# Sixteen sequences of a state-space scan: fourteen of them in a hardware loop, or all sixteen written out

## The chip, the cores and the metric

The kernel runs on one core of a Trainium2 chip. The metric is the device time of one execution in microseconds (us). The core has five instruction streams that run side by side and meet only at semaphores: PE (TensorE, matmuls), DVE (VectorE), ACT (ScalarE), POOL (GpSimd) and SP (SyncE, which here only issues DMA transfers).

## The reference, cut to what matters

A batch of 16 sequences of 1024 tokens (256 features each) passes through a Mamba layer and then through an attention layer with a mixture of experts. Only the Mamba layer, the state space, is touched here:

```python
xz = einsum('bld,ed->ble', hidden_states, in_proj_w)          # 512 channels x, 512 channels z
x_conv = silu(sum(x_pad[:, w:w + L] * conv_w[:, w] for w in range(4)) + conv_b)
dt_in, Bv, Cv = split(einsum('bld,ed->ble', x_conv, x_proj_w))  # 64, 16 and 16 columns
delta = softplus(einsum('blr,dr->bld', dt_in, dt_proj_w) + dt_proj_b)
def step(h, inp):                                             # over the 1024 tokens of a sequence
    d_t, B_t, C_t, u_t = inp
    h = h * exp(d_t[:, :, None] * A) + (d_t * u_t)[:, :, None] * B_t[:, None, :]
    return h, einsum('bdn,bn->bd', h, C_t)                    # 16 states for each of 512 channels
y = (ys + x_conv * D) * silu(z)
out = x + einsum('bld,md->blm', y, out_proj_w)
```

## The kernel before, in words

Four stages follow each other with a barrier between them: `mamba_stage`, `attention_stage`, `routing_stage`, `expert_stage`. The change is in the first alone.

`mamba_stage` works on a sequence in two halves of 512 tokens, called r = 0 and 1; a pair (sequence, half) is the `q` of the code. In a half there are 32 units: two passes over 256 channels each, times 16 states. A unit holds two scans of 128 channels by 512 tokens. For a unit, SP fetches a row of B (`m_bb`) and a row of C (`m_cb` or `m_cv`), broadcast to 128 partitions; ACT makes `m_decay` = exp(delta * A) (line 524); POOL multiplies `m_du` by the row of B (`m_dbu`, line 373); DVE runs the recurrence as two scans (`m_h`, line 634), in the second half from the saved end `m_h_end` of the first; POOL (13 units of 32, line 382) or DVE (19 of 32, line 616) multiplies the state by the row of C (`m_prod`); PE adds the products up in `m_y_bank` (line 751). Four units are in flight (`RING = 4`). The projections, the convolution, the softplus and the output of the neighbouring halves are cut into small pieces and put between the units by a table (`SIDE`), on the same engines: `m_side`, `m_xc`, `m_zs`, `m_delta`, `m_xres`.

What belongs to which turn is counted by semaphores: `count(q, per_block, done)` (lines 46 to 50) gives the number that a semaphore must have reached in half q. Each engine runs the same function `sequences` (lines 233 to 238): its body once for sequence 0, then in a loop on the engine (`Fori`) for sequences 1 to 14, then once for sequence 15. In the loop b is a value in a register, so the numbers that are waited for are worked out in registers (`REGISTER_ALU` at lines 58 and 65) and so are the addresses of the transfers. For sequences 0 and 15 they are constants. Four helpers wait through `wait_apart`, which puts an increment of a semaphore that nobody reads behind the wait: all waits of SP, one of ACT (line 474) and one of DVE (line 555).

The loop is closed by a compare and a branch back to its first instruction; 14 passes have 13 such jumps back. Loop passes are entered from sequence 0 and left to sequence 15 without one. A sequence is named here by its number; it begins for DVE with the first scan whose input is not `m_h_end`.

Of the kernel before, what the change touches and what calls it, by code (L numbers as in the profile page):

```python
# [13 lines left out]
S, L, H = 16, 1024, 256  # L14
# [16 lines left out]
class Allocator:  # L31
# [11 lines left out]
    def sem(self, name):  # L43
        return self.ctx.enter_context(self.nc.semaphore(self.prefix + name))


def count(block, per_block, done):


    b, half = block  # L50
    return b * (HALVES * per_block) + (half * per_block + done)


def wait(eng, sem, value):

    if isinstance(value, int) and value <= 0:
        return
    eng.wait_ge(sem, value)


def wait_apart(eng, sem, value, passed):

    if isinstance(value, int) and value <= 0:
        return
    eng.wait_ge(sem, value)
    eng.sem_inc(passed, 1)


def mamba_stage(nc, x, w, x1, rows_bc):
# [25 lines left out]
    OUTS, PREPS = len(out_uses), len(prep_uses)  # L95
# [17 lines left out]
    def prep_done(kind, i):  # L113

        return 1 + prep_uses.index((kind, i))

    def bank_of(kind, i):
        return uses.index((kind, i)) % SIDE_BANKS
# [16 lines left out]
    with ExitStack() as ctx:  # L135
        al = Allocator(nc, ctx, "m_")
        sb, sem = al.sb, al.sem
# [47 lines left out]
        s_const = sem("const")  # L185
        s_a = sem("a")
        s_diag = sem("diag")
        dve_passed, sp_passed = sem("dve_passed"), sem("sp_passed")
        act_passed = sem("act_passed")
        x_loaded = sem("x_loaded")  # L190
        xres_loaded = sem("xres_loaded")
        x1_stored = sem("x1_stored")
# [3 lines left out]
        stats_done = sem("stats_done")  # L196
# [3 lines left out]
        prep_taken = sem("prep_taken")  # L200
# [27 lines left out]
            return (q[0], q[1] + 1) if q[1] < HALVES - 1 else (q[0] + 1, 0)  # L228

        def first(q):  # L230
            return isinstance(q[0], int) and q[0] == 0 and q[1] == 0

        def sequences(eng, body):

            body(0, False)
            with eng.Fori(1, S - 1) as b:
                body(b, False)
            body(S - 1, True)

        def unit_at(q, u):  # L240

# [11 lines left out]
        @block.sync  # L253
        def _(sp):
            def wait_then(sem_, value):
                wait_apart(sp, sem_, value, sp_passed)

            def load_x(q):
                if not first(q):
                    wait_then(ln_done, count(q, 1, 0))  # L260
                sp.dma_start(xin[:], x_blocks[q[0], q[1]]).then_inc(x_loaded, 16)
# [50 lines left out]
            def body(b, last):  # L312
                for half in range(HALVES):
                    q = (b, half)
                    ends = last and half == HALVES - 1
                    for u in range(UNITS):
                        if u + RING - 1 < UNITS or not ends:
                            load_b(*unit_at(q, u + RING - 1))
                        to, later = unit_at(q, u + 2)
                        if later in POOL_UNITS and not (ends and to is not q):  # L320
                            load_c(to, POOL_UNITS.index(later))
                        if later in VECTOR_UNITS and not (ends and to is not q):
                            load_c_for_vector(to, VECTOR_UNITS.index(later))
                        if first(q) and u + 1 in POOL_UNITS and u == 0:
                            load_c(q, 0)
                        if u == 0 and not last:
                            load_x(after(after(q)))
                        if u == 1 and not first(q):
                            load_residual(before(q))
                        if u == STORE_ROWS_AT and not ends:  # L330
                            store_rows(after(q))
                        if u == UNITS - 3 and not first(q):
                            store_result(before(q))
            sequences(sp, body)
            g = (S - 1, HALVES - 1)
            load_residual(g)
# [5 lines left out]
        def _(pool):  # L342
# [8 lines left out]
            def inverse_deviation(q):  # L351
                wait(pool, stats_done, count(q, 2, 2))
                wait(pool, ln_done, count(q, 1, 0))
                nc.gpsimd.tensor_tensor(rstd[:], moments[:, :, 1], eps[:], ALU.add).then_inc(rstd_done, 1)
                nc.gpsimd.tensor_tensor(shift[:], moments[:, :, 0], minus_one[:], ALU.mult).then_inc(rstd_done, 1)
                wait(pool, rstd_done, count(q, 4, 2))
                nc.gpsimd.tensor_tensor(rstd[:], rstd[:], minus_half[:], ALU.pow).then_inc(rstd_done, 1)
                wait(pool, rstd_done, count(q, 4, 3))
                nc.gpsimd.tensor_tensor(shift[:], shift[:], rstd[:], ALU.mult).then_inc(rstd_done, 1)
# [53 lines left out]
        def _(act):  # L413
# [57 lines left out]

            def softplus_exp(q, i):
                bank = side_bank[:, bank_of("dt", i)]
                wait_apart(act, prep_taken, count(q, PREPS, prep_done("dt", i)), act_passed)
                if i == 0:
                    nc.scalar.preload_act_table_set("natural_log_exp_and_others")
                nc.scalar.activation(bank, bank, ACT.Exp, scale=-1.0).then_inc(soft_done, 1)
# [55 lines left out]
            def body(b, last):  # L533
                for half in range(HALVES):
                    scan_block((b, half), last and half == HALVES - 1, not last)
            sequences(act, body)


        @block.vector
        def _(dve):  # L540
# [8 lines left out]
            def statistics(q):  # L549
                wait(dve, x_loaded, count(q, 16, 16))  # L550
                wait(dve, rstd_done, count(q, 4, 0))
                for j in range(TB):
                    ins = nc.vector.bn_stats(stats[:, j], xin[:, j])
                ins.then_inc(stats_done, 1)
                wait_apart(dve, stats_done, count(q, 2, 1), dve_passed)
                for j in range(TB):
                    ins = nc.vector.bn_aggr(moments[:, j], stats[:, j])
                ins.then_inc(stats_done, 1)
# [60 lines left out]
            def scan_block(q, last, norm):  # L619
                r = q[1]  # L620
                for u in range(UNITS):
                    n, slot = u % NS, u % RING
                    for cc in range(PC):
                        wait(dve, decay_done, scans_done(q, u, cc))
                        if cc == 0:
                            wait(dve, dbu_done, units_done(q, u))
                            to, earlier = unit_at(q, u - RING)
                            if not (first(q) and u < RING):
                                wait(dve, prod_by_pool, count(to, PU, pool_upto(earlier)))
                            if r:  # L630
                                wait(dve, end_saved, q[0] * UNITS + min(UNITS, UNITS - RING + u + 1))
                            else:
                                wait(dve, end_saved, q[0] * UNITS + (u - RING + 1 if u >= RING else 0))
                        nc.vector.tensor_tensor_scan(h[:, slot, cc], decay[:, cc], dbu[:, slot, cc],  # L634
                                                     h_end[:, u, cc:cc + 1] if r else 0.0,
                                                     ALU.mult, ALU.add).then_inc(scan_done, 1)
                        if cc == 0:
                            to, earlier = unit_at(q, u - 1)
                            if earlier in VECTOR_UNITS and not (first(q) and u == 0):
                                weigh_state(to, earlier)  # L640
                        finishing(q, PC * u + cc, not first(q))
                        if not last:
                            preparation(q, PC * u + cc, norm)
# [5 lines left out]
            def body(b, last):  # L649
                for half in range(HALVES):  # L650
                    scan_block((b, half), last and half == HALVES - 1, not last)
            sequences(dve, body)
            q = (S - 1, HALVES - 1)
# [1090 lines left out]
def build(nc, t, out):  # L1744


    def scratch(name, shape):
        return nc.dram_tensor(name, shape, F32, kind="Internal").ap()

    x1 = scratch("x1", (S, L, H))  # L1750
    n2 = scratch("n2", (TOKENS, H))
    logits = scratch("logits", (L // P, P, S, EXPERTS))
    info = scratch("info", (P * COLS, 2))
    rows_bc = scratch("rows_bc", (HALVES, 2, NS, T))
    mamba_stage(nc, t["x"], t, x1, rows_bc)
    attention_stage(nc, x1, t, out, n2, logits)
    with nc.sbuf_tensor("weight_row", [P, NB], I32) as weight_row:
        routing_stage(nc, logits, info, weight_row)
        expert_stage(nc, t, n2, info, weight_row, out)
# [36 lines left out]
```

## Time and profile before

| what | value |
|---|---|
| device time, median of 3 runs (lowest to highest) | 6873.41 us (6872.57 to 6882.47) |
| time of the profiled execution | 6878.51 us |
| span of the profiled execution, on which all rows stand | 6876.8 us |
| instructions executed | 90070 |
| busy: PE, POOL, DVE, ACT | 88%, 77%, 60%, 51% |
| first scan of sequence 0, of 1, of 15 on DVE | 73.75, 298.17, 3544.91 us |
| first work of DVE in the attention stage | 3787.77 us |

The profiled execution took 1.7 us more than its span and 5.1 us more than the median. The busy shares are means over four stages. The state space fills the first 3780 us or so, a little more than half of the span; the digits of the page show DVE and POOL at 9 tenths there, PE at 8 to 9 and ACT at 6 to 7.

### The profile page before, as it was taken

The numbers are of one execution on the slowest core, as the hardware profiler recorded it, in microseconds if no ns is written. First come the engines' busy times: TensorE is split into PE (matmuls) and PEld (weight loads), VectorE is DVE, ScalarE is ACT, GpSimd is POOL, SyncE is SP. The second block draws the span as 40 slices with busy tenths as digits, with TensorE's granted clock in tenths as the row PEclk, the third lists the DMA queues.
The fourth block names the chain that finished last, engine by engine and source line by source line (L and its number), as shares of the span: only waits on it lengthen the run. The fifth ranks groups of instructions, "written<-read, shape, count | busy, mean of one in ns | idle before, by whom it ended". The sixth has DMA issues, their size and how long they took to land. (4 is left out here: it accounts for less than half of the span.)

```text
span 6876.8 us, 90070 instructions
## 1 busy us (share of the span) xinstructions
PE 6057.5 (88%) x24804; PEld 3848.5 (56%) x24804; DVE 4131.6 (60%) x4999; ACT 3516.7 (51%) x6417; POOL 5285.1 (77%) x4084
## 2 busy tenths in 40 slices
PE   7999989998989998999897899930299999999999
PEld 3444434443434443444443688830288888888888
DVE  6999999989999999999998477750000000000000
ACT  6676667666666666666665688720022222222222
POOL 6999999999999999999998777637655555555554
PEclk9999999999999999999999999965699999999999
DMA  3554555555554554455554244410266666666654
GB/s 124 163 161 161 159 160 161 157 153 163 160 161 156 160 163 157 157 162 160 161 158 142 73 123 125 125 60 1 76 183 183 184 184 184 185 185 185 180 168 132
DMA packets 556960, 1030.16 MB, mean 150 GB/s; under 512 B 82546, under 2 KB 250996, under 8 KB 521904
## 3 DMA queue, kind: packets, MB, share of 16 engines
q1 hardware_dynamic: 441168, 669.34, 31.4%
q0 software_dynamic: 115296, 355.56, 17.5%
q8 instruction: 146, 2.39, 0.1%
q14 instruction: 350, 2.87, 0.1%
HBM read 926.04 MB, written 88.88 MB: 148 GB/s over the span
## 5 line engine op out<-in xcount | busy, mean ns | idle before, releaser
L373 POOL TENSOR_TENSOR m_dbu<-m_du,m_bb 128x1024 f32<-128x1024 f32 x1024 | 2395.0, 2369 | 55.3 <-DVE m_h L634 54.6
L751 PE MATMUL m_y_bank<-m_prod,m_ident 128*128 128x512 f32 x4096 | 1955.6, 606 | 157.2 <-POOL m_prod L382 153.8
L524 ACT ACTIVATE m_decay<-m_delta,m_a_neg 128x512 f32<-128x512 f32 x2048 | 1417.6, 694 | 916.0 <-DVE m_h L634 893.5
L751 PEld LDWEIGHTS m_y_bank<-m_prod,m_ident 128*128 128x128 f32 x4096 | 778.4, 193 | 1125.9 <-issue 900.5
L634 DVE TENSOR_TENSOR_SCAN m_h<-m_decay,m_dbu 128x512 f32<-128x512 f32 x1024 | 1198.2, 1210 | 107.3 <-issue 76.9
L634 DVE TENSOR_TENSOR_SCAN m_h<-m_decay,m_h_end,m_dbu 128x512 f32<-128x512 f32 x1024 | 1261.0, 1274 | 0.7
L1694 DVE TENSOR_SCALAR e_ye<-e_ybank,e_listing 128x256 f32<-128x256 f32 x270 | 118.3, 480 | 1818.7 <-PE e_ybank L1728 1818.7
L1680 ACT ACTIVATE e_a<-e_ubank 128x512 f32<-128x512 f32 x540 | 322.4, 597 | 1474.9 <-PE e_ubank L1719 1474.9
L382 POOL TENSOR_TENSOR m_prod<-m_h,m_cb 128x1024 f32<-128x1024 f32 x416 | 983.8, 2365 | 90.5 <-DVE m_h L634 83.2
L1719 PE MATMUL e_ubank<-e_xT,e_w 128*128 128x256 f32 x4320 | 979.5, 380 | 1.3 <-ACT e_xT L1671 1.3
L1728 PE MATMUL e_ybank<-e_w,e_a 128*128 128x256 f32 x4320 | 954.5, 379 | 0.7 <-ACT e_a L1680 0.7
L1728 PEld LDWEIGHTS e_ybank<-e_w,e_a 128*128 128x128 f32 x4320 | 820.7, 190 | 112.6 <-ACT e_a L1680 1.1
L1719 PEld LDWEIGHTS e_ubank<-e_xT,e_w 128*128 128x128 f32 x4320 | 812.2, 191 | 107.1 <-issue 1.6
L1624 POOL DMA_INDIRECT e_w<-in_w,weight_row x270 | 258.4, 957 | 782.0 <-PE e_ybank L1728 734.7
L616 DVE TENSOR_TENSOR m_prod<-m_h,m_c_bank 128x1024 f32<-128x1024 f32 x608 | 730.1, 1201 | 36.6 <-ACT m_c_bank L511 34.7
L718 PE MATMUL m_side<-m_xnT,m_w_in 128*128 128x512 f32 x1024 | 547.3, 640 | 104.6 <-ACT m_xnT L440 86.6
L1641 POOL DMA_INDIRECT out<-e_ye,e_token x270 | 430.1, 1593 | 111.0 <-issue 81.4
L723 PE MATMUL m_side<-m_xpad,m_tap_diag 128*128 128x512 f32 x1024 | 495.7, 592 | 0.0
L718 PEld LDWEIGHTS m_side<-m_xnT,m_w_in 128*128 128x128 f32 x1024 | 205.3, 206 | 398.7 <-issue 237.1
L1706 PE MATMUL e_tbank<-e_ident,e_xe 128*128 128x128 f32 x540 | 81.5, 274 | 369.0 <-DMA e_xe<-n,e_token 369.0
L511 ACT COPY m_c_bank<-m_cv 128x512 f32<-128x512 f32 x608 | 358.5, 590 | 83.6 <-DVE m_prod L616 82.5
L1457 POOL DMA_INDIRECT info<-r_entry,r_slot_of x256 | 250.9, 980 | 133.8 <-issue 80.4
(198 smaller groups left out, 6532.1 us busy)
## 6 DMA issues: line engine op xcount, KB each, us to landing
m_bb<-rows_bc SPq DMA_DIRECT2D x1024, 256.0 KB, 3.7
m_cv<-rows_bc SPq DMA_DIRECT2D x608, 256.0 KB, 3.8
m_cb<-rows_bc SPq DMA_DIRECT2D x416, 256.0 KB, 3.4
m_xin<-in_x SPq DMA_DIRECT2D x32, 512.0 KB, 5.4
m_xres<-in_x SPq DMA_DIRECT2D x32, 512.0 KB, 5.5
x<-m_xres SPq DMA_DIRECT2D x32, 512.0 KB, 6.0
a_xa<-x SPq DMA_DIRECT2D x64, 256.0 KB, 2.9
a_xr<-x SPq DMA_DIRECT2D x64, 256.0 KB, 3.2
```

The source lines that it names most:

```text
L373: nc.gpsimd.tensor_tensor(dbu[:, slot], du[:, q[1], p * PC:(p + 1) * PC], bb[:, slot].unsqueeze(1).to_broadcast([P, PC, T]), ALU.mult).the ...
L382: nc.gpsimd.tensor_tensor(prod[:, slot], h[:, slot], cb[:, C_BUFFER[k]].unsqueeze(1).to_broadcast([P, PC, T]), ALU.mult).then_inc(prod_by_ ...
L511: nc.scalar.copy(c_bank[:], cv[:, V_BUFFER[k]]).then_inc(c_copied, 1)
L524: nc.scalar.activation(decay[:, cc], delta[:, r, c], ACT.Exp, scale=a_neg[:, c, n:n + 1]).then_inc(decay_done, 1)
L616: nc.vector.tensor_tensor(prod[:, slot], h[:, slot], c_bank[:].unsqueeze(1).to_broadcast([P, PC, T]), ALU.mult).then_inc(prod_by_vector, 1)
L634: nc.vector.tensor_tensor_scan(h[:, slot, cc], decay[:, cc], dbu[:, slot, cc], h_end[:, u, cc:cc + 1] if r else 0.0, ALU.mult, ALU.add).th ...
L718: ins = nc.tensor.matmul(bank, w_in[:, piece, col:col + P], xnT[:, piece], start=(piece == 0), stop=final)
L723: ins = nc.tensor.matmul(bank, tap_diag[:, i, piece], xpad[:, i, piece:piece + T], start=(piece == 0), stop=final)
L751: ins = nc.tensor.matmul(y_bank[:, cc], ident[:], prod[:, slot, cc], start=False, stop=(n == NS - 1))
L1641: nc.gpsimd.indirect_dma_start(out, bass.IndirectOffsetOnAxis(ap=token[:, col:col + 1], axis=0), ye[:, n % Y_RING, j], None, compute_op=AL ...
L1719: ins = nc.tensor.matmul(ubank[:, (n * UG + g) % U_RING, i], w1[:, r, k, c * P:(c + 1) * P], xT[:, n % 2, k], start=(k == 0), stop=(k == K ...
L1728: ins = nc.tensor.matmul(ybank[:, n % 2, j], a[:, n % 2, c, j * P:(j + 1) * P], w2[:, n % W_RING, c], start=(c == 0), stop=(c == FC - 1))
```

## The change

The loop is gone. Each engine's body is called 16 times by Python, with b an integer, so all 16 sequences (each a pair of half blocks) stand in the program one after the other. All numbers that are waited for and all addresses are constants, so the register arithmetic is gone too, and `wait_apart` with its increments and its three semaphores is replaced by `wait`.

```diff
@@ -53,17 +53,9 @@
 def wait(eng, sem, value):
 
-    if isinstance(value, int) and value <= 0:
+    if value <= 0:
         return
     eng.wait_ge(sem, value)
-
-
-def wait_apart(eng, sem, value, passed):
-
-    if isinstance(value, int) and value <= 0:
-        return
-    eng.wait_ge(sem, value)
-    eng.sem_inc(passed, 1)
@@ -185,8 +177,6 @@
-        dve_passed, sp_passed = sem("dve_passed"), sem("sp_passed")
-        act_passed = sem("act_passed")
@@ -228,14 +218,12 @@
         def first(q):
-            return isinstance(q[0], int) and q[0] == 0 and q[1] == 0
+            return q == (0, 0)
 
         def sequences(eng, body):
 
-            body(0, False)
-            with eng.Fori(1, S - 1) as b:
-                body(b, False)
-            body(S - 1, True)
+            for b in range(S):
+                body(b, b == S - 1)
@@ -253,7 +241,7 @@
             def wait_then(sem_, value):
-                wait_apart(sp, sem_, value, sp_passed)
+                wait(sp, sem_, value)
@@ -471,7 +459,7 @@
-                wait_apart(act, prep_taken, count(q, PREPS, prep_done("dt", i)), act_passed)
+                wait(act, prep_taken, count(q, PREPS, prep_done("dt", i)))
@@ -552,7 +540,7 @@
-                wait_apart(dve, stats_done, count(q, 2, 1), dve_passed)
+                wait(dve, stats_done, count(q, 2, 1))
```

The program's own order of work stays: the same operations stand in the same order on each engine. Two places show what changes between them. On DVE, this is the end of sequence 0 and the first rows of the loop before (scans at line 634, product at line 616):

```order
L570 SCALAR_TENSOR_TENSOR m_zs<-m_tanh,m_side 128x512 [waits m_prep_taken]
L236 UNCONDITIONAL_BRANCH
L236 ISA
L58 ISA [waits m_decay_done]
L58 ISA [waits m_dbu_done]
L58 REGISTER_ALU [waits m_prod_by_pool]
L634 SCALAR_TENSOR_TENSOR m_h<-m_decay,m_dbu 128x512 [waits m_end_saved]
L58 REGISTER_ALU
L634 SCALAR_TENSOR_TENSOR m_h<-m_decay,m_dbu 128x512 [waits m_decay_done]
```

and this the end of the loop's body, with the jump back, and the first row of sequence 15:

```order
L634 SCALAR_TENSOR_TENSOR m_h<-m_decay,m_h_end,m_dbu 128x512 [waits m_decay_done]
L58 REGISTER_ALU
L570 SCALAR_TENSOR_TENSOR m_zs<-m_tanh,m_side 128x512 [waits m_prep_taken]
L236 REGISTER_ALU
L236 COMPARE_AND_BRANCH
L634 SCALAR_TENSOR_TENSOR m_h<-m_decay,m_dbu 128x512 [waits m_prod_by_pool,m_end_saved,m_dbu_done,m_decay_done]
```

After the change the turn from sequence 0 to 1 on DVE reads so (its line 558 is line 570 of before, 622 is 634, 604 is 616):

```order
L558 SCALAR_TENSOR_TENSOR m_zs<-m_tanh,m_side 128x512 [waits m_prep_taken]
L622 SCALAR_TENSOR_TENSOR m_h<-m_decay,m_dbu 128x512 [waits m_prod_by_pool,m_end_saved,m_dbu_done,m_decay_done]
L622 SCALAR_TENSOR_TENSOR m_h<-m_decay,m_dbu 128x512 [waits m_decay_done]
L622 SCALAR_TENSOR_TENSOR m_h<-m_decay,m_dbu 128x512 [waits m_prod_by_pool,m_end_saved,m_dbu_done,m_decay_done]
L604 TENSOR_TENSOR m_prod<-m_h,m_c_bank 128x1024 [waits m_summed,m_c_copied,m_scan_done]
```

No branch is left at any of the 15 turns, and the waits sit on the operations themselves. On SP, which issues the transfers, the loop's head before is:

```order
L285 DMA m_cb<-rows_bc 128x512 [waits m_prod_by_pool]
L236 UNCONDITIONAL_BRANCH
L236 ISA
L280 DMA m_bb<-rows_bc 128x512 [waits m_dbu_done]
L65 ISA
L291 DMA m_cv<-rows_bc 128x512 [waits m_c_copied]
L65 ISA
L261 ISA [waits m_ln_done]
L261 DMA m_xin<-in_x 128x4x256
```

and now:

```order
L273 DMA m_cb<-rows_bc 128x512 [waits m_prod_by_pool]
L268 DMA m_bb<-rows_bc 128x512 [waits m_dbu_done]
L279 DMA m_cv<-rows_bc 128x512 [waits m_c_copied]
L249 DMA m_xin<-in_x 128x4x256 [waits m_ln_done]
```

The transfers stand in the same order with the same waits; what stood between them is gone. Per pass the loop held 542 written instructions on DVE, 508 on ACT, 281 on SP and 240 on POOL. The written program grows on DVE from 2445 to 4850 rows and on SP from 961 to 2611.

## Rows read from the trace of the kernel before

**Rows 1.** Page, parts 1 and 5: span, busy time, the scans and what preceded them.
```profile
span 6876.8 us, 90070 instructions
PE 6057.5 (88%) x24804; PEld 3848.5 (56%) x24804; DVE 4131.6 (60%) x4999; ACT 3516.7 (51%) x6417; POOL 5285.1 (77%) x4084
...
L634 DVE TENSOR_TENSOR_SCAN m_h<-m_decay,m_dbu 128x512 f32<-128x512 f32 x1024 | 1198.2, 1210 | 107.3 <-issue 76.9
L634 DVE TENSOR_TENSOR_SCAN m_h<-m_decay,m_h_end,m_dbu 128x512 f32<-128x512 f32 x1024 | 1261.0, 1274 | 0.7
```

**Rows 2.** Timeline of DVE at the first jump back; start, length, idle before in brackets.
```profile
523.25 0.67 DVE L570 SCALAR_TENSOR_TENSOR m_zs<-m_tanh,m_side 128x512 f32<-128x512 f32 x1
531.36 2.34 DVE L634 TENSOR_TENSOR_SCAN m_h<-m_decay,m_dbu 128x512 f32<-128x512 f32 x2 [7.43 <-issue]
```

**Rows 3.** Timeline of DVE: the turn with the longest and with the shortest idle.
```profile
2624.68 2.34 DVE L634 TENSOR_TENSOR_SCAN m_h<-m_decay,m_dbu 128x512 f32<-128x512 f32 x2 [8.35 <-issue]
...
2855.44 3.45 DVE L634 TENSOR_TENSOR_SCAN m_h<-m_decay,m_dbu 128x512 f32<-128x512 f32 x3 [6.38 <-POOL m_dbu L373]
```

**Rows 4.** Timeline of DVE where the loop is entered and where it is left.
```profile
297.59 0.67 DVE L570 SCALAR_TENSOR_TENSOR m_zs<-m_tanh,m_side 128x512 f32<-128x512 f32 x1
298.17 2.34 DVE L634 TENSOR_TENSOR_SCAN m_h<-m_decay,m_dbu 128x512 f32<-128x512 f32 x2
...
3544.33 0.67 DVE L570 SCALAR_TENSOR_TENSOR m_zs<-m_tanh,m_side 128x512 f32<-128x512 f32 x1
3544.91 1.23 DVE L634 TENSOR_TENSOR_SCAN m_h<-m_decay,m_dbu 128x512 f32<-128x512 f32 x1
```

**Rows 5.** Windows: stretch, its length, busy time and instructions of each engine, clock, DMA.
```profile
298.17:523.93 225.76, 210.18 (x513) 95.06 (x512) 216.03 (x219) 155.22 (x280) 220.83 (x103) 0.98 0.53 163
3320.45:3544.91 224.46, 207.95 (x504) 94.48 (x505) 216.05 (x219) 156.65 (x282) 214.57 (x100) 0.97 0.51 154
73.75:298.17 224.42, 205.97 (x472) 90.22 (x473) 213.43 (x216) 157.64 (x284) 219.87 (x103) 0.95 0.51 162
182.17:298.17 116.00, 108.76 (x265) 49.22 (x264) 109.57 (x111) 77.19 (x127) 112.67 (x53) 0.97 0.52 163
410.17:523.93 113.76, 105.63 (x258) 47.65 (x257) 109.69 (x110) 75.47 (x124) 110.98 (x52) 0.98 0.52 161
3790.00:4460.00 670.00, 646.16 (x6943) 553.58 (x6944) 448.29 (x1018) 508.04 (x985) 488.80 (x1288) 0.99 0.38 110
```

**Rows 6.** Waits of DVE in 298.17 to 523.9: total us, times, longest.
```profile
DVE m_xres L584 <- PE m_side L707: 5.9, 4, 1.7
DVE m_prod L616 <- ACT m_c_bank L511: 2.3, 2, 1.3
```

**Rows 7.** Timeline of POOL at the turns 0 to 1 and 1 to 2.
```profile
292.42 6.97 POOL L373 TENSOR_TENSOR m_dbu<-m_du,m_bb 128x1024 f32<-128x1024 f32 x3
...
518.10 6.97 POOL L373 TENSOR_TENSOR m_dbu<-m_du,m_bb 128x1024 f32<-128x1024 f32 x3
...
533.78 2.35 POOL L373 TENSOR_TENSOR m_dbu<-m_du,m_bb 128x1024 f32<-128x1024 f32 x1 [4.10 <-DVE m_h L634]
```

**Rows 8.** Timeline of ACT behind the turn 1 to 2, then of the same place at 14 to 15.
```profile
537.10 0.69 ACT L524 ACTIVATE m_decay<-m_delta,m_a_neg 128x512 f32<-128x512 f32 x1 [0.47 <-DVE m_h L634]
...
3550.64 0.69 ACT L524 ACTIVATE m_decay<-m_delta,m_a_neg 128x512 f32<-128x512 f32 x1 [0.47 <-DVE m_h L634]
```

**Rows 9.** Waits of DVE, sequence 0's second half, then 3790 to 4460 (longest).
```profile
DVE m_zs L578 <- PE m_y_bank L751: 2.2, 1, 2.2
DVE m_prod L616 <- issue: 1.3, 1, 1.3
...
DVE a_hid L1209 <- PE a_side L1336: 101.6, 45, 2.4
```

**Rows 10.** Page, part 3: the queues that bring instructions: packets, MB, share.
```profile
q8 instruction: 146, 2.39, 0.1%
q14 instruction: 350, 2.87, 0.1%
```

## The prediction

> **What bounds the kernel now.** I read the busy shares first: PE leads over the whole span [rows 1], but that is a mean over four stages and the change touches only the first. So I cut that stage into sequences at DVE's first scan and asked for the busy time in each stretch. In sequence 1 DVE is busy 216.03 of 225.76 us, POOL 220.83, PE 210.18, ACT 155.22 [rows 5]. Three engines are nearly full, and the scans tie them together. The waits inside the sequence are small: DVE waits 5.9 us for PE's output bank and 2.3 us for ACT's copy of C [rows 6], and never for POOL.
>
> The timeline of DVE shows one thing that is not small. At the jump back from the loop's end to its head DVE ends its last gate at 523.92 and starts the next scan at 531.36, with 7.43 us idle that the profile gives to "issue" or to nobody in particular [rows 2]. There are 13 such places, with idle times from 6.38 to 8.35 us [rows 3]; one by one they add up to 95.3 us, which is nearly all of the 107.3 us of idle time in front of the first half's scans [rows 1]. At three of the 13 POOL's product is named as the releaser, as at 2855.44, with the same length; POOL jumps back too. Where the loop is entered (0 to 1) and where it is left (14 to 15) DVE runs through with no idle time at all [rows 4]. The same work stands on both sides of all 15 turns; what the two quiet ones lack is the jump back.
>
> **The change part by part.**
>
> *The jumps.* They go, on all five engines at once, so every turn should look like the two quiet ones. The question is what follows a quiet turn: the idle time of DVE also lets POOL and PE catch up, and part of the 95.3 us may be given back as waits inside the sequence. The trace holds one sequence with a quiet turn in front of it that does all the work of a middle one: sequence 1, from 298.17 to 523.93, 225.76 us [rows 5]. It is also a steady state. At the quiet turn 0 to 1 DVE starts its scan 5.75 us after POOL began its run of three products (298.17 - 292.42), and at the end of sequence 1 it stands 5.82 us after the same run (523.93 - 518.10) [rows 7]: POOL's lead has not changed, and POOL itself took 518.10 - 292.42 = 225.68 us for the round. So I expect sequences 2 to 14 each to repeat sequence 1.
>
> Now: from 298.17 to 3544.91 is 3246.74 us for 14 sequences [rows 4]. Then: 14 x 225.76 = 3160.64 us. The difference is 86.1 us. Put the other way, 95.3 us of stops go and 9.2 us come back, since the gap lets PE and POOL get ahead and the sequence behind it runs shorter, as sequence 14 does in 224.46 us [rows 5].
>
> Bounds of this term. If nothing came back and all 14 ran like sequence 14, it would be 3246.74 - 14 x 224.46 = 104.3 us. The other end is the quiet turn followed by a slower sequence: unrolled code in the trace has a second half of 116.00 us, in sequence 0, against 113.76 us in sequence 1 [rows 5]. I read this as POOL's backlog and not as the code: the first half of sequence 0 has no output to finish and DVE runs through it in 108.42 us (182.17 - 73.75, the starts of the windows in rows 5), faster than POOL can follow, and then waits 2.2 us for PE's sum, which waits for POOL [rows 9]. If it were the code after all, 14 second halves would cost 14 x 2.24 = 31.4 us, both halves 62.7 us; the gain would be 23 to 55 us. I take 86.1, because it comes from the row that is the same work in the same state.
>
> *Register arithmetic and the extra increments.* In a pass DVE drops about 320 of 542 written instructions, and the others drop as many or fewer. I cost this at nothing. Behind the turn 1 to 2 an exponential of ACT waits 0.47 us for its scan, with the wait in a register (537.10); at the same place behind 14 to 15, with a constant, it waits 0.47 us again (3550.64) [rows 8]. What hides it is the engine's own work: DVE's operations last 0.67 to 2.4 us each, so the stream is read ahead of them. Cover gone, a cost would have shown as idle time in front of every scan, and there is 0.7 us over 1024 scans of the second halves [rows 1]. It could be a gain of that 0.7 us at most, and no loss since instructions only go.
>
> *SP.* Its transfers keep order and waits. After a jump SP is late as well, but POOL waits for DVE there (4.10 us at 533.78 [rows 7]) and for no transfer. Nothing to gain, and a later product or row of B would have shown in that row. Zero.
>
> *Fetching the longer program.* The instruction queues moved 2.39 + 2.87 = 5.26 MB for 90070 instructions [rows 1, 10], some 58 bytes for each one executed and far more than the few times ten thousand written ones would take once; so the loop is fetched again on each pass already, and writing it out adds no traffic. Straight-line code also runs faster than this elsewhere: from 3790 to 4460 DVE takes 1018 instructions in 670 us, 1.5 per us against 219 in 225.76, 0.97 per us, and PE 6943 [rows 5], and DVE's longest total wait there is for PE [rows 9], with no stop of the turn's kind. I cost it at nothing.
>
> The Trainium skill, "Runtime: NRT & Kernel Launch", section Instruction fetch mechanics, says that instructions are prefetched in order in blocks of 16 KiB, that a jump outside the two blocks held forces a fetch first, and that passing from block to block is mostly hidden. Its "Advanced Engine Details and Errata", Control Flow Timing, on the other hand gives a compare-and-branch about 108 ns: by that figure 13 jumps would be worth an estimated 1.4 us and the change nothing. The trace has 7.43 us at the jump and sides with the first.
>
> *Sum.* -86.1 us on the profiled 6878.5, that is 6792.4. The median of the runs is 5.1 us lower, so 6873.4 - 86.1 = 6787.3; I say 6787.
>
> **The rivals.**
>
> B, nothing comes back: the gain is 104.3 us, 6769. For it: sequence 14, in front of a quiet turn, takes 224.46 us. Against it: it starts behind a stop, and sequence 1, which does not, takes 225.76.
>
> C, written-out code is slower per half than looped code by the 2.24 us of sequence 0: gain 23 to 55 us, 6818 to 6850. For it: sequence 0 is the only full unrolled second half. Against it: the wait for PE's sum explains it.
>
> D, the stop does not belong to the jump, but to the turn of a sequence in general, and the two quiet turns are chance: 6873, no change. Against it: 13 of 13 jumps have it, 0 of 2 turns without one. The cheap-branch figure above leads here too. The case in which the change does not do what it says is this one.
>
> E, slower: the stream must be refilled, and the jump only fixes where the stop falls. In straight-line code a refill that comes too late would stop DVE once or more per sequence, at a place where POOL and PE have no lead to lose. The price is that of the stop, 7.43 us, and it decides from 86.1 / 14 = 6.15 us per sequence: one stop each gives 14 x 7.43 = 104.0, less 86.1, so 6891; two give 6995. For it: one unexplained stop of 1.3 us in sequence 0 [rows 9]. Against it: the 670 us of attention at a higher rate.
>
> **How the numbers follow.** A 70%, B 12%, C 8%, D 5%, E 5%. Within A the spread is the sequence's length: the 13 looped sequences before 14 take, without their stops, (3320.45 - 298.17 - 95.3) / 13 = 225.15 us on the mean, 0.6 less than sequence 1; as much to either side of 225.76 gives gains of 95 and 78 us, 6779 to 6796. The range reaches to B on one side and to the near end of C on the other: 6764 to 6820, which leaves out most of C, D and E, about 15%. A measurement of this kernel tells 0.2% from no change, about 14 us: A, B and C are faster by more (90%), D is no change (5%), E is slower (5%).
>
> **What would show it.** In the new profile: no idle time of several us in front of the first scan of any sequence; starts of sequences 225 to 226 us apart, sequence 15 at about 3459 us; DVE's waits for PE's output bank four per sequence and near 5.9 us; POOL busy near 98% of the stage; the later stages as long as before. The idle total in front of the first half's scans falls from 107.3 to about 12 us. The forecast is wrong if idle "issue" time of DVE turns up elsewhere in the stage (E), if the turns keep their stop (D), or if starts are 228 us or more apart without stops (C).

## The result and the profile after

The changed kernel takes 6782.73 us (median of 4 runs, 6781.93 to 6783.45) against 6875.41 us for the kernel before in the same comparison (4 runs, 6872.57 to 6882.47). The ratio is 0.9864 with a 95% interval of 0.9847 to 0.9881: faster by 1.4%, or 92.7 us. The forecast was 6787 us in a range of 6764 to 6820.

The page of the changed kernel, its head and the lines that answer to [rows 1] and [rows 10]:

```profile
span 6781.4 us, 77307 instructions
...
PE 6024.3 (89%) x24804; PEld 3839.4 (57%) x24804; DVE 4123.4 (61%) x4999; ACT 3517.1 (52%) x6417; POOL 5284.3 (78%) x4084
...
q8 instruction: 199, 3.26, 0.2%
q14 instruction: 204, 1.67, 0.1%
...
L622 DVE TENSOR_TENSOR_SCAN m_h<-m_decay,m_h_end,m_dbu 128x512 f32<-128x512 f32 x1024 | 1255.4, 1265 | 1.7 <-ACT m_decay L512 1.7
...
L622 DVE TENSOR_TENSOR_SCAN m_h<-m_decay,m_dbu 128x512 f32<-128x512 f32 x1024 | 1193.8, 1203 | 8.8 <-ACT m_decay L512 8.3
```

The numbers of operations are the same on every engine; 12763 other instructions are gone, and the busy times hardly move. What moves is the idle time in front of the scans of the first halves: 107.3 us before, 8.8 us now.

The timeline of DVE in the changed kernel at three turns, 1 to 2, 2 to 3 and 14 to 15 (start, length):

```profile
522.03 0.66 DVE L558 SCALAR_TENSOR_TENSOR m_zs<-m_tanh,m_side 128x512 f32<-128x512 f32 x1
522.61 2.33 DVE L622 TENSOR_TENSOR_SCAN m_h<-m_decay,m_dbu 128x512 f32<-128x512 f32 x2
...
747.57 0.66 DVE L558 SCALAR_TENSOR_TENSOR m_zs<-m_tanh,m_side 128x512 f32<-128x512 f32 x1
748.15 2.33 DVE L622 TENSOR_TENSOR_SCAN m_h<-m_decay,m_dbu 128x512 f32<-128x512 f32 x2
...
3450.96 0.65 DVE L558 SCALAR_TENSOR_TENSOR m_zs<-m_tanh,m_side 128x512 f32<-128x512 f32 x1
3451.53 2.32 DVE L622 TENSOR_TENSOR_SCAN m_h<-m_decay,m_dbu 128x512 f32<-128x512 f32 x2
```

No scan has a bracket of idle time. Turn 1 to 2 had 7.43 us [rows 2], and it now looks like the entry and the exit of the loop did [rows 4]. The windows of sequences 1, 3 and 14 (stretch, length, busy time and instructions by engine, clock, DMA), which answer to [rows 5]:

```profile
297.08:522.61 225.53, 210.08 (x513) 95.14 (x512) 215.50 (x219) 156.93 (x283) 220.72 (x103) 0.98 0.50 164
748.15:972.93 224.78, 211.16 (x513) 95.93 (x512) 215.68 (x219) 156.93 (x283) 220.53 (x103) 0.98 0.50 164
3226.00:3451.53 225.53, 210.08 (x513) 95.16 (x512) 215.50 (x219) 156.93 (x283) 220.65 (x103) 0.98 0.49 162
```

From 297.08 to 3451.53 the sequences 1 to 14 take 3154.45 us, 225.32 each. They had taken 3246.74 [rows 4]: 92.3 of the 95.4 us by which the span shrank. Another 1.1 us went ahead of sequence 1 and 2.0 behind the start of sequence 15.

### The profile page after: what moved, and what is told of

Its sections match the earlier page's. It is cut to its first block and busy times, and to the rows that moved or that the text cites. A ratio compares the mean times of both kernels' runs of the same rounds, so it can differ in the third digit from the quotient of the medians.

```text
span 6781.4 us, 77307 instructions
## 1 busy us (share of the span) xinstructions
PE 6024.3 (89%) x24804; PEld 3839.4 (57%) x24804; DVE 4123.4 (61%) x4999; ACT 3517.1 (52%) x6417; POOL 5284.3 (78%) x4084
## 3 DMA queue, kind: packets, MB, share of 16 engines
q8 instruction: 199, 3.26, 0.2%
q14 instruction: 204, 1.67, 0.1%
## 5 line engine op out<-in xcount | busy, mean ns | idle before, releaser
L706 PE MATMUL m_side<-m_xnT,m_w_in 128*128 128x512 f32 x1024 | 524.3, 616 | 23.8 <-DVE m_delta L596 17.9
```

What stands on the lines that cost most here:

```text
L706: ins = nc.tensor.matmul(bank, w_in[:, piece, col:col + P], xnT[:, piece], start=(piece == 0), stop=final)
```

## The experiments

Each ratio is against runs of the kernel before on the same chip, 6872 to 6874 us (median); the changed kernel's 6783 us and most steps from one experiment to another compare runs on different chips. "Stop" is the idle time of DVE from its last gate of a sequence until 7 us into the next, added up from the timeline and divided by the number of jumps (13, or 6 for pairs; by 13 turns where DVE has no loop). "q14" is the packets of the second instruction queue; the first has 146 where PE keeps its loop (217 for pairs) and 199 where PE is written out.

| kernel | engines with a loop | time, us | stop, us | q14 |
|---|---|---|---|---|
| before | all five | 6874 | 7.3 | 350 |
| changed | none | 6783 | 0 | 204 |
| loop_dve | DVE | 6820.5 | 2.7 | 256 |
| loop_others | SP, POOL, ACT, PE | 6786.9 | 1.0 | 283 |
| loop_pool | POOL | 6786.0 | 0 | 185 |
| loop_pool_pad | POOL, body longer by 320 | 6785.3 | 0 | 284 |
| loop_dve_act | DVE, ACT | 6813.4 | 2.4 | 301 |
| loop_dve_sp | DVE, SP | 6842.5 | 4.5 | 309 |
| loop_dve_act_sp | DVE, ACT, SP | 6842.3 | 5.1 | 355 |
| pairs | all five, two sequences a pass | 6814.2 | 6.6 | 346 |
| before_late | all five, x loads moved | 6829.3 | 4.1 | 350 |
| loop_dve_late | DVE, x loads moved | 6804.3 | 2.0 | 256 |
| after_late | none, x loads moved | 6785.2 | 0 | 204 |

**Which engine's jump costs the time.** The edit lets each engine choose whether it loops; where waits are constants no unread increment follows them. By this DVE has four instructions fewer in front of its loop than in the kernel before; the increments inside its loop stay.

```diff
-        def sequences(eng, body):
+        LOOPED = ("DVE",)                    # loop_others: ("SP", "POOL", "ACT", "PE"), and so on
+        def sequences(name, eng, body):
+            if name not in LOOPED:
+                for b in range(S):
+                    body(b, b == S - 1)
+                return
             body(0, False)
             with eng.Fori(1, S - 1) as b:
                 body(b, False)
             body(S - 1, True)
```

DVE alone in a loop. 

> Only DVE keeps its loop over sequences 1 to 14 (register waits, 13 jumps back); the other four engines are written out. Theory 1, the stop at a turn is DVE's own jump, paid on DVE: the 13 stops of about 7.4 us stay and the time is 6870 to 6880 us, as before. Theory 2, DVE's stop is handed down by the jump of another engine (POOL, ACT or SP late behind its own jump): DVE passes the turns with under 1 us and the time is 6783 to 6790 us. Theory 3, the stop needs all five to jump at once: something between, near 6830 us.

Measured: 6820.5 us (6813.1 to 6828.2), ratio 0.9925 (0.9909 to 0.9942). The time lies between theories 1 and 2; it is near the figure of theory 3, but that asked for all five jumps, and here one does it: DVE's own jump costs 38 of the 92 us. The four others in a loop. 

> DVE is written out, SP, POOL, ACT and PE keep their loops. Theory 1: no stop of DVE's own; ACT and POOL each stop at their jump, but are one to three operations ahead of DVE (ACT's exponentials are two ahead, POOL's products two units), so most is covered: 0 to 3 us a turn, 6783 to 6822 us. Theory 2: the stops stay near 7.4 us and the time is 6870 to 6880 us.

Measured: 6786.9 us (6781.0 to 6787.9), ratio 0.9872 (0.9855 to 0.9888): 4 us. So the time needs DVE's jump; the jumps of the other four are covered, in the way that theory 1 says, as long as DVE does not jump. But the parts, 38 and 4, do not add up to the 92 of all five together. The timeline of DVE at the turn 2 to 3, with DVE alone in the loop:

```profile
751.92 0.66 DVE L577 SCALAR_TENSOR_TENSOR m_zs<-m_tanh,m_side 128x512 f32<-128x512 f32 x1
753.81 2.34 DVE L641 TENSOR_TENSOR_SCAN m_h<-m_decay,m_dbu 128x512 f32<-128x512 f32 x2 [1.23 <-POOL m_dbu L380]
757.86 1.22 DVE L641 TENSOR_TENSOR_SCAN m_h<-m_decay,m_dbu 128x512 f32<-128x512 f32 x1 [1.71 <-ACT m_h_end L513]
```

The stop is there but falls into two short ones, 2.9 us in all, where the kernel before had one of 7.30 us at the same turn. The releasers named can't be the reason, since POOL and ACT are the same engines that keep DVE waiting for nothing at this place in the changed kernel.

The register rows and branches of DVE (marked `DVEq`), which the timeline leaves out, show why there are two. Here they are for this turn: the branch, the first instruction of the loop, and its ninth (how many; shortest, median and longest in ns; first and last start in us).

```profile
L243 DVEq COMPARE_BRANCH  x1: 63/63/63, 749.3 to 749.3; - x1
L243 DVEq FUSED_REGOPS  x1: 63/63/63, 753.4 to 753.4; - x1
...
L58 DVEq ALU_OP  x1: 40/40/40, 757.7 to 757.7; - x1
```

DVE takes the branch at 749.3, while its last operations still run, and takes no further instruction for 4.1 us. Then it takes eight instructions, two scans among them, and stops again: the ninth comes 4.3 us after the first. The profile's DMA part has one packet of the second instruction queue in each of the two stretches, 749.3 to 753.4 and 753.4 to 757.7:

```profile
q14 instruction: 1, 0.01, 1.2%
...
q14 instruction: 1, 0.01, 0.5%
```

The same holds for all 13 turns of this kernel: two packets between the branch and the ninth instruction, and each time DVE goes on 0.8 to 1.6 us after a packet has landed. So a jump costs two waits for code, one behind the other: one for the head of the loop, one where the code that came with it ends.

**Is it the number of jumps or the arithmetic in registers?** Two sequences in a pass, which leaves the register waits as they are.

```diff
-            with eng.Fori(1, S - 1) as b:
-                body(b, False)
+            with eng.Fori(0, (S - 2) // 2) as pair:
+                body(pair * 2 + 1, False)
+                body(pair * 2 + 2, False)
```

> The loop on all engines has 7 passes of two sequences each, so 6 jumps back in place of 13, and the register arithmetic stays as before. If the jumps carry the whole difference: 6783 + 6/13 x 92.7 = 6826 us, with 6 stops of about 7.4 us on DVE. If the register arithmetic or the turn of a sequence carries it, the time stays at 6870 to 6880 us.

Measured: 6814.2 us (6813.0 to 6821.0), ratio 0.9917 (0.9901 to 0.9934), six stops of 4.4 to 8.0 us, and none at the turns inside a pass, where all waits are still in registers. The direction is that of the jumps; the time is 12 us under the forecast, since two of the six stops are short and the sequences, in front of a stop and behind it, are mostly shorter than the changed kernel's, so that a stop costs about 31.4 / 6 = 5.2 us. Sequence 1, with all its waits in registers and a quiet turn at both ends, takes 224.4 us (296.51 to 520.87), not more than the 225.5 us of the changed kernel: register arithmetic on DVE costs nothing that shows.

**Does a short body make the jump free?** POOL alone in a loop. 

> Only POOL keeps its loop, whose body of 240 instructions is the shortest of the five. If every jump stops its engine for about 7.4 us whatever the length of the body, POOL, which is busy 220.8 of 225.3 us in a sequence, falls 7.4 us behind at each turn with 4.5 us of slack to make it up: 13 x 3 to 13 x 5 us more than written out, 6820 to 6850 us. If its lead of two units covers the stop, or a short body makes no stop: 6783 to 6790 us.

Measured: 6786.0 us (6782.7 to 6789.9), no stop on DVE, and 19 packets fewer on the queue than with POOL written out. DVE's sequences start 224.3 to 226.0 us apart, as in the changed kernel. Then the same with a longer body:

```diff
                     ALU.mult).then_inc(dbu_done, 1)
+                for k in range(5):
+                    pool.sem_inc((dve_passed, sp_passed, act_passed)[(u + k) % 3], 1)
```

> As the kernel in which only POOL keeps its loop, with five increments of semaphores that nobody reads behind each product m_dbu, 320 more in the body, which had 240 listed instructions and caused no stop (6786 us, 185 packets on queue 14 against 204 when written out). Theory 1, a jump is free when the body is short enough to be held on the engine: the longer body is fetched anew, queue 14 moves 13 x 4 to 13 x 6 more packets, and POOL stops at each turn, 2 to 5 us each, of which its lead covers a part: 6790 to 6830 us. Theory 2, POOL's jump is covered by its lead whatever the length: 6783 to 6790 us.

Measured: 6785.3 us (6784.1 to 6787.3). The queue moves 99 packets more than without the increments, 7.6 for each jump (a few of them for the increments in sequences 0 and 15): the longer body is fetched again on each pass, the short one is not. But the time does not move, so for the time theory 2 holds here: a jump on POOL is covered, held or not. 5120 more instructions on an engine that is busy 98% of the stage cost nothing either. That tests the extra increments of the term "register arithmetic at zero", for POOL; it isn't a test of register arithmetic.

**Whose jump makes DVE's longer?** 

> DVE and ACT keep their loops, POOL, PE and SP are written out. Alone, DVE's loop cost 38 us over all written out (two stops of about 1.1 and 1.7 us at most turns), that of the four others 4 us, all five together 92. Theory 1, engines that jump at the same time fetch their code one behind the other, so the waits add up: 20 to 50 us more than DVE alone, 6840 to 6870 us, with DVE's stops growing to 5 us and more. Theory 2, the jumps are independent and only the latest counts: 6820 to 6825 us.

Measured: 6813.4 us (6801.7 to 6824.3), ratio 0.9916 (0.9899 to 0.9932), stop 2.4 us. ACT adds nothing (the ranges of the two kernels overlap); theory 1, that every fetch lengthens every other, falls. 

> DVE and SP keep their loops. SP's transfers come late behind its jump (4 to 9 us gaps in its row of transfers), but POOL has rows of B and C in hand. Theory 1, fetches queue up behind each other whoever makes them: like DVE with ACT, 6840 to 6870 us. Theory 2, ACT is the partner that matters, since DVE waits for its exponentials and nobody waits for SP: 6820 to 6825 us.

Measured: 6842.5 us (6839.2 to 6848.1), ratio 0.9956 (0.9939 to 0.9972), stop 4.5 us. SP adds 22 us. That is inside theory 1's range, but theory 1 gave ACT the same, and ACT adds nothing; theory 2 had SP at zero. The timeline shows what SP's jump does. DVE and SP (queue of transfers), turn 2 to 3, with DVE and SP in loops:

```profile
750.19 0.66 DVE L577 SCALAR_TENSOR_TENSOR m_zs<-m_tanh,m_side 128x512 f32<-128x512 f32 x1
754.03 2.34 DVE L641 TENSOR_TENSOR_SCAN m_h<-m_decay,m_dbu 128x512 f32<-128x512 f32 x2 [3.18 <-issue]
759.14 1.23 DVE L641 TENSOR_TENSOR_SCAN m_h<-m_decay,m_dbu 128x512 f32<-128x512 f32 x1 [2.77 <-POOL m_dbu L380]
```

```profile
746.50 0.40 SPq L268 DMA_DIRECT2D m_xin<-in_x  x1
```

and SP with DVE alone in a loop, where DVE's last gate starts at 751.92:

```profile
745.35 0.43 SPq L268 DMA_DIRECT2D m_xin<-in_x  x1
```

SP issues at each turn the load of a new half of x, `m_xin`, and one unit later the residual `m_xres`, 512 KB each. With SP written out `m_xin` is issued 6.6 us before DVE's last gate, with SP in a loop 3.7 us before. Between the two kernels the stop is longer where the loads are nearer: 2.7 us at 6.2 to 6.6, 4.5 us at 3.2 to 3.9 (within one kernel this isn't seen). That suggested that the code which DVE has to fetch waits behind these transfers.

**Move the transfers.** In three kernels the two loads go from units 0 and 1 to units 6 and 9 of each half; nothing else changes.

```diff
-                        if u == 0 and not last:
+                        if u == 6 and not last:
                             load_x(after(after(q)))
-                        if u == 1 and not first(q):
+                        if u == 9 and not first(q):
                             load_residual(before(q))
```

> The kernel before, all five loops, with the two transfers of 512 KB that SP issues around every turn (m_xin at unit 0, m_xres at unit 1) moved to units 6 and 9. In the traces so far DVE's stop at a turn goes with the moment of m_xin before DVE's last gate: 6.6 us before, stop 3; 3.4 to 3.8 us before, stop 4.5 to 8. Theory 1, the code fetched after the jump queues behind these transfers: the stop falls from 7.3 us to 3 or less, the time to 6783 to 6830 us. Theory 2, it depends on how many engines jump together and not on the data: the stops stay at 7 us, 6868 to 6880 us.

Measured: 6829.3 us (6826.8 to 6844.5), ratio 0.9943 (0.9926 to 0.996). The stops fall from 7.3 to 4.1 us, not to 3 or less; the time falls by 44 us, inside theory 1's bounds, with the whole loop still there. The timeline of DVE in this kernel at two turns:

```profile
1443.54 3.45 DVE L634 TENSOR_TENSOR_SCAN m_h<-m_decay,m_dbu 128x512 f32<-128x512 f32 x3 [4.97 <-issue]
...
3039.14 0.66 DVE L570 SCALAR_TENSOR_TENSOR m_zs<-m_tanh,m_side 128x512 f32<-128x512 f32 x1
3041.82 3.45 DVE L634 TENSOR_TENSOR_SCAN m_h<-m_decay,m_dbu 128x512 f32<-128x512 f32 x3 [2.02 <-POOL m_dbu L373]
```

The longest stop that is left is 4.97 us, the shortest 2.02. 

> Only DVE keeps its loop, with the same two transfers moved to units 6 and 9. Theory 1: the stops of 2 to 3 us fall to under 1 us, the time from 6820 to 6783 to 6795 us. Theory 2: unchanged, 6813 to 6828 us.

Measured: 6804.3 us, but its four runs lie between 6790.8 and 6814.5, so the step from 6820.5 is in the right direction and its size is not well known. The stops fall only from 2.7 to 2.0 us: theory 1 had them under 1. A part of DVE's stop has nothing to do with the loads of x: from the branch to the loop's first instruction it is 4.0 us on the mean here, against 3.7 us with the loads at the turn; what gets shorter is the way to the ninth, 3.5 against 4.5 us. 

> The changed kernel with the same two transfers moved: a control, since it has no jump. Theory 1 and 2 both: within 5 us of 6783 us. A gain of more than 5 us would mean that the transfers cost time at the turn even without a jump.

Measured: 6785.2 us (6781.8 to 6786.4), ratio 0.9872 (0.9856 to 0.9889), as expected: without a jump the place of the loads is worth nothing. So their 44 us in the looped kernel come through the jump. Last, three engines. 

> DVE, ACT and SP keep their loops, POOL and PE are written out. DVE with SP had 6843 us and stops of 4 to 6 us, DVE with ACT 6813 us and stops of 2 to 3 us, all five 6874 us and stops of 7.4 us. If SP's jump (which puts m_xin later) and ACT's fetch add up to the full stop, 6865 to 6876 us. If POOL's or PE's jump is needed for the rest, 6840 to 6850 us.

Measured: 6842.3 us (6837.5 to 6853.9), ratio 0.9952 (0.9936 to 0.9969), in the range of the second case: ACT adds nothing again, and 31 us are left to the kernel before. But they don't need POOL's or PE's jump. The branch and the loop's first instruction on DVE in the kernel before, turn 1 to 2:

```profile
L236 DVEq COMPARE_BRANCH  x1: 63/63/63, 520.6 to 520.6; - x1
L236 DVEq FUSED_REGOPS  x1: 63/63/63, 526.0 to 526.0; - x1
```

Here four instructions follow, all on registers, and the fifth is the first scan, at 531.36 [rows 2]. So the second wait for code begins in front of the first scan, and not behind two scans as in the kernels that left four increments out ahead of the loop. Means over the 13 turns, from the branch to the loop's first instruction and from there to the first one behind the second wait:

| kernel | branch to head, us | head to second restart, us | instructions between | stop, us |
|---|---|---|---|---|
| before | 5.36 | 5.27 | 4 | 7.3 |
| before, second profile | 5.07 | 5.16 | 4 | 6.9 |
| loop_dve_act_sp | 5.38 | 5.17 | 8 | 5.1 |
| loop_dve_sp | 4.87 | 5.10 | 8 | 4.5 |
| loop_dve | 3.67 | 4.50 | 8 | 2.7 |
| before_late | 3.61 | 3.80 | 4 | 4.1 |

The two waits are as long with three loops as with five; what differs is that two scans of 1.15 us run during the second one. By an estimate they are worth 13 x 2.3 = 30 of the 31 us; the stop itself differs by 1.8 to 2.2 us. A kernel with all five loops and the four increments left out, which would test this by its time, wasn't run.

**The kernel before once more.** 

> The kernel before, word for word, for a second profile. In the first the scans took 1210 and 1274 ns, in all kernels since 1203 to 1206 and 1264 to 1265. If this belongs to the kernel with the loop on all engines, the second profile has 1210 and 1274 again; if it belongs to the chip or the moment, it has 1203 to 1206 and 1265, and the time is 2 to 8 us below the first median.

Measured: 6872.9 us, span 6870.6. The scans in its profile:

```profile
L634 DVE TENSOR_TENSOR_SCAN m_h<-m_decay,m_dbu 128x512 f32<-128x512 f32 x1024 | 1195.7, 1205 | 103.2 <-issue 45.8
L634 DVE TENSOR_TENSOR_SCAN m_h<-m_decay,m_h_end,m_dbu 128x512 f32<-128x512 f32 x1024 | 1255.4, 1264 | 0.8
```

1205 and 1264 ns in place of 1210 and 1274: the longer scans belonged to the first profiled execution, not to the loop. Its 13 stops run from 6.0 to 8.0 us, 90.0 us in all, so the stop itself is a property of the kernel.

**What follows.** A stop needs DVE's jump, and it is two waits for code: in the kernel before 5.4 us from the branch to the loop's head and 5.3 us from there to the first scan, of which the operations that DVE already had cover 3.3 us. With DVE's loop alone the two are 3.7 and 4.5 us, and two scans run in between. Loads of x beside the turn make both longer (5.4 and 5.3 against 3.6 and 3.8 us with the loads moved); SP's loop, which brings these loads nearer, does so too, but SP with its loads moved wasn't run. The remaining difference between three loops and five is the place of the loop's head in the fetched code, and hardly any of it is left that would need POOL or PE. That a jump makes DVE wait for code is shown by the branch, the packets that land and the instructions that follow them. Why the packet comes only 1.0 to 2.7 us after the branch in loop_dve, and whether it is the loads of x that it waits for, no row shows.

## Why the prediction was right

*The place.* It said that DVE's idle time at the 13 jumps is what goes, and it sided with a fetch of code as what a jump costs; the packets that land behind each branch bear that out, though they come in two waits and not in one. The idle time before the first halves' scans fell from 107.3 to 8.8 us (12 forecast), and no turn has a stop.

*What comes back.* This was the step with the most in it: not 95.3 us but 86.1, because a sequence behind a quiet turn is longer than one behind a stop. Measured on the same stretch: 92.3 us, so 3.0 us come back and not 9.2. Against the second profile of the kernel before, whose scans are as short as the changed kernel's, it is 3243.00 (3540.41 - 297.41) less 3154.45, that is 88.6 of 90.0 us of stops, and 1.4 us come back. So this step was right in its sign and too large in its size, and the time of 6787 was near in part because the term is small beside the 90 us of stops. The looped sequences 1 to 13 without their stops take 225.15 us on the mean in the first profile and 225.28 in the second; the changed kernel's take 225.30. Only sequence 14 is clearly longer behind a quiet turn, 225.53 against 224.46 and 224.33. I had priced all 14 by sequence 1 of one profile, 225.76 us. In the second profile of the same kernel sequence 1 takes 224.94, and in the changed kernel it isn't a fixed point either: three times two sequences of 225.5 us are followed by one of 224.8, and once one of 226.0 by one of 224.3 (the forecast had 225 to 226 for all). I had taken the state to be the same for ever. Over sequence 1 DVE slid by 0.07 us against POOL, and I called that nothing; that the slide is what ends each run of 225.5 isn't shown.

*Waits inside the sequence.* DVE's waits in sequence 1 of the changed kernel, to be held against [rows 6]:

```profile
DVE m_xres L572 <- PE m_side L695: 6.4, 4, 1.8
DVE m_prod L604 <- ACT m_c_bank L499: 1.4, 1, 1.4
DVE m_prod L604 <- issue: 1.3, 1, 1.3
```

Four waits for PE's output bank as forecast, 6.4 us where 5.9 was said. The unexplained 1.3 us in front of a product, on which rival E leaned, now comes once in each sequence. It is no refill of the stream: in sequence 1 the looped kernel has the same wait at the same place, with ACT's copy of C named; in the changed kernel too that copy ends at 446.47, 0.09 us before the product starts. The two rows of DVE's timeline, before and then after:

```profile
447.78 1.22 DVE L616 TENSOR_TENSOR m_prod<-m_h,m_c_bank 128x1024 f32<-128x1024 f32 x1 [1.25 <-ACT m_c_bank L511]
```

```profile
446.56 1.22 DVE L604 TENSOR_TENSOR m_prod<-m_h,m_c_bank 128x1024 f32<-128x1024 f32 x1 [1.30 <-issue]
```

*Register arithmetic at zero.* Held: the turns inside a pass of pairs have no stop with all waits in registers, sequence 1 there is no longer than written out, and 5120 extra increments on POOL cost nothing. No kernel was run that changes DVE's arithmetic alone. And the increments matter in a way that I didn't look for: with four of them ahead of DVE's loop the second wait for code falls before two scans, and without them behind.

*Longer program at zero.* Held: no stop turned up elsewhere. The reason given was half right. The queues moved 5.26 MB before and 3.26 + 1.67 = 4.93 MB after, so writing out did not add traffic; but I said that the loop is fetched again on each pass, which is true of DVE (52 packets more with its loop) and wrong for PE, whose queue moves 53 packets more, not fewer, when it is written out, and for POOL's short body. The rule of the Trainium skill that I cited ("Runtime: NRT & Kernel Launch", Instruction fetch mechanics) makes a jump fetch only where its target isn't in the two blocks held. POOL's 240 instructions and then 560 agree with it in their packets. Where it has blocks of 16 KiB, the packets of the second queue are 8.2 KB each here (1.67 MB in 204), and each of DVE's two waits in loop_dve has one of them.

*SP at zero.* True for the change as a whole, but its working was incomplete: with DVE's loop, SP's adds 22 us, most likely through the time at which it issues the loads of x, which no step of mine looked at.

*The rivals.* B (all 104.3 us, 6769) did not come. C (2.24 us a half slower) fell: second halves of written-out sequences take 113.6 us (522.61 - 408.97, their first scans), not 116.0, while sequence 0 again takes 116.0 (297.08 - 181.04); the surplus was sequence 0's own. D and E fell: 15 turns without a stop and none elsewhere.

## What to carry to other kernels

Before you price a loop on the engines, look at its jump back on the engine that has no slack, and look for a place in the same trace that does the same work without the jump; take the stretches without the jump from more than one profile, since one sequence of 225.76 us here was 224.94 in the next. The engines that ran ahead of DVE hid their own jumps: with DVE alone written out the time was within 4 us of the changed kernel, so it may be enough that the bound engine does not jump. And where a loop must stay, keep large transfers away from its turn: here that alone brought 44 of the 92 us. Look also at how many long operations stand between the loop's head and the second wait for code: two scans more there go with some 30 us less over 13 jumps.

## What was not expected of the hardware

The cost of a jump is not a constant of the engine: DVE's stop was 2.0 to 2.7 us with only its own loop, 4.5 with SP's beside it, 7.3 with all five, and 4.1 with all five and two loads of 512 KB moved away from the turn. One jump makes two waits for code, of 3.7 and 4.5 us in the case of DVE's loop alone, and the second can fall a few instructions into the loop. Four instructions of no effect in front of the loop move that place. Some kernels whose DVE jumps scatter more from run to run (24 us between the fastest and slowest of four for loop_dve_late, 23 for loop_dve_act, 15 for loop_dve) than the one with no jump (1.5 us); the kernel before, whose DVE jumps too, had 4.5 us over 13 runs on one chip and 9.9 over 4 in the first comparison.
